# One matmul for two outputs of a spectral filter: 36 blocks in place of 48

## What is computed

```python
def _stu_conv(phi, u, n):
    sgn = jnp.where(jnp.arange(sl) % 2 == 0, 1.0, -1.0)
    ...
    U_plus = irfft(Vf[None, :, :, None] * Uf_p[:, :, None, :])[:, :sl]
    U_minus = irfft(Vf[None, :, :, None] * Uf_m[:, :, None, :])[:, :sl]
    U_minus = U_minus * sgn[None, :, None, None]

def _compute_spectral(u, sigma, phi, Mpp, Mpm):
    U_plus, U_minus = _stu_conv(phi, u, PADDED_SL)
    s = sigma ** SIGMA_POW
    out = jnp.einsum('btkd,k,kde->bte', U_plus, s, Mpp)
    return out + jnp.einsum('btkd,k,kde->bte', U_minus, s, Mpm)
```

## Time and profile before

| | us |
|---|---|
| median of three runs (3904.05 to 3920.32) | 3916.36 |
| the profiled execution, span from the first to the last instruction | 3932.8 |
| PE busy | 3385.7 |
| DVE busy | 2484.0 |
| POOL busy | 1702.7 |
| ACT busy | 1442.3 |
| matmuls of L1599, 3072 of them, busy | 507.5 |

### The profile page before, as it was taken

One profiled execution on the slowest core, in us unless ns is written; L12 is line 12 of the kernel. 1 busy time (PEld: TensorE's weight loads), 2 busy tenths in 40 slices (PEclk: granted clock), 3 DMA queues, 4 the chain that ended last, 5 costly groups with the idle time before them and its releaser, 6 DMA issues. The chain is left out here.

```text
span 3932.8 us, 69093 instructions
## 1 busy us (share of the span) xinstructions
PE 3385.7 (86%) x21387; PEld 2365.0 (60%) x21387; DVE 2484.0 (63%) x4247; ACT 1442.3 (37%) x2188; POOL 1702.7 (43%) x1424
## 2 busy tenths in 40 slices
PE   6336999999999999999999999999999569999998
PEld 1124555555555555555555555555555359898887
DVE  2346666676666767666766766667676556464646
ACT  0002333333333333333333333333333235454545
POOL 0464555555555555555555555555555320000000
PEclk8557999999999999999999999999999779999999
DMA  2524454445545544444554445455555624333333
GB/s 78 165 85 138 120 133 127 131 125 129 137 119 133 135 126 128 130 132 118 138 134 124 126 129 136 120 132 135 125 130 124 136 70 135 101 133 102 119 123 103
DMA packets 289629, 487.77 MB, mean 124 GB/s; under 512 B 95336, under 2 KB 113144, under 8 KB 289304
## 3 DMA queue, kind: packets, MB, share of 16 engines
q1 hardware_dynamic: 257160, 398.26, 36.8%
q0 software_dynamic: 32400, 88.52, 9.4%
HBM read 258.31 MB, written 23.27 MB: 72 GB/s over the span
## 5 line engine op out<-in xcount | busy, mean ns | idle before, releaser
L1108 ACT ACTIVATE attention_probs<-attention_pss 128x896 f32<-128x896 f32 (+4 forms) x768 | 623.0, 811 | 1320.9 <-PE attention_pss L957 1310.4
L1165 DVE TENSOR_REDUCE attention_mx<-attention_pss 128x2 f32<-128x1024 f32 (+3 forms) x520 | 525.5, 1022 | 377.8 <-PE attention_pss L970 208.1
L1041 PE MATMUL attention_psY<-attention_probs,attention_xt 128*64 128x128 f32 (+7 forms) x4386 | 733.5, 440 | 2.1 <-DMA attention_xt<-xt 1.8
L1283 POOL DMA_INDIRECT attention_gat<-table,attention_idx x585 | 559.8, 957 | 191.6 <-issue 118.8
L954 PE MATMUL attention_pss<-attention_QA,attention_KA 128*128 128x512 f32 (+4 forms) x1536 | 554.1, 416 | 49.5 <-ACT attention_probs L1108 43.7
L1696 DVE SCALAR_TENSOR_TENSOR spectral_eo<-spectral_psE,spectral_sig,spectral_eo 64x512 fp32r<-64x512 f32 x512 | 383.9, 750 | 263.8 <-ACT spectral_eo L1675 259.2
L1264 POOL TENSOR_TENSOR attention_nat_l<-attention_qk,attention_nat_h 128x512 fp32r<-128x512 f32 x260 | 425.3, 1636 | 259.3 <-ACT attention_nat_h L1127 259.3
L970 PE MATMUL attention_pss<-attention_nat_h 64*128 64x512 f32 (+2 forms) x1560 | 350.7, 451 | 201.7 <-DVE attention_mx L1165 198.2
L1599 PE MATMUL spectral_psE<-spectral_tz,spectral_up 128*128 128x256 f32 (+2 forms) x3072 | 507.5, 324 | 4.3 <-DVE spectral_eo L1696 4.3
L1256 POOL TENSOR_TENSOR attention_qk<-attention_tA,attention_tB 128x512 f32<-128x512 f32 x260 | 411.1, 1592 | 203.5 <-DVE attention_tB L1180 201.9
L1599 PEld LDWEIGHTS spectral_psE<-spectral_tz,spectral_up 128*128 128x128 f32 x3072 | 470.7, 188 | 44.9 <-DVE spectral_eo L1696 6.1
(11 more groups left out here) (194 smaller groups left out, 3862.4 us busy)
## 6 DMA issues: line engine op xcount, KB each, us to landing
attention_QA<-attention_nat_h SPq DMA_DIRECT2D x520, 128.0 KB
spectral_tz<-phis SPq DMA_DIRECT2D x128, 320.5 KB, 4.7
spectral_tz<-phis SPq DMA_DIRECT2D x128, 320.0 KB, 4.3
attention_xb<-xn SPq DMA_DIRECT2D x66, 512.0 KB, 4.0
attention_wt<-wsplit SPq DMA_DIRECT2D x66, 512.0 KB, 5.9
attention_KA<-attention_nat_h SPq DMA_DIRECT2D x260, 128.0 KB
attention_KB<-attention_nat_h SPq DMA_DIRECT2D x260, 128.0 KB
attention_KA<-attention_nat_l SPq DMA_DIRECT2D x260, 128.0 KB
```

The costliest lines, as they stand in the source:

```text
L1041: ins = pe.matmul(psY[C * half:C * half + C, c0:c1], xt[:, kt_, :], probs[:, q + c0:q + c1], start=first, stop=(j == NS - 1), skip_group_c ...
L1108: act.activation(probs[:, pstep[j]:pstep[j] + width], pss[:, slot, lead:lead + width], ACT.Exp, scale=float(E) ** -0.5).then_inc(s_act, 1)
L1165: ins = dve.tensor_reduce(mx_far[:, :, i - 4] if k0 else mx[:, :, i], scores, AX.X, ALU.max)
L1283: pool.indirect_dma_start(gat[:, n, :, :].rearrange("p q c -> p (q c)"), None, d.table.rearrange("r q c -> r (q c)"), bass.IndirectOffsetO ...
```

## The change

The two outputs that take their tokens from the same parity have the same stationary operand. One matmul now makes both of them: its moving operand is a stretch of the even taps' rows and one of the odd taps' rows, and its output is two runs in one PSUM bank. So that both fit a bank, it holds only half of the positions of each output. A unit `u = 2 * src + half` stands in the place of the output `e`: `half` 0 is positions 0 to 255, `half` 1 the rest. A unit of `half` 0 needs the token blocks 0 and 1, one of `half` 1 all four; the last block of each has 128 columns of each output, the others 256.

For this `tz` keeps the two tap parities in one row, `LAGS` apart, and the odd ones are read one element later where `src` is 0. `phases` gives the places in `eo` that the two halves of a bank belong to; `eo` itself and `mix_in` are as before. The number of instructions of ACT and DVE, their sizes, the loads and the semaphores with their counts are the same.

```diff
+LAGS = P + HB + 2
...
-        tz = sb("tz", [P, 2, 2, 2, P + HB + 1], F32R)
+        tz = sb("tz", [P, 2, 2, 2 * LAGS + 2], F32R)
...
+        def phases(k, u, rows, b):
+            src, half = u // 2, u % 2
+            flat = eo[rows, k % 2, :, :, b, 2 * P * half:2 * P * half + 2 * P].rearrange("q o p n -> q (o p) n")
+            return flat[:, 0:4:3, :] if src == 0 else flat[:, 1:3, :]
...
-                                sp.dma_start(tz[:, k % 2, part, odd, 0:n].bitcast(F32),
+                                sp.dma_start(tz[:, k % 2, part, odd * LAGS:odd * LAGS + n].bitcast(F32),
...
-                        for e in range(4):
-                            odd, p = e // 2, e % 2
-                            pe.wait_ge(s_lo, 64 * g + 4 * k + e + 1)
-                            src = p if not odd else 1 - p
-                            off = P + (1 if odd and p == 1 else 0)
+                        for u in range(4):
+                            src, half = u // 2, u % 2
+                            pe.wait_ge(s_lo, 64 * g + 4 * k + u + 1)
+                            wide = LAGS + 1 - src
                             for n, (x, y) in enumerate(((0, 0), (0, 1), (1, 0))):
-                                for a in range(4):
-                                    first = min(P * a, HB - 2 * P)
-                                    lag = off + first - P * a
-                                    ins = pe.matmul(psE[:, e, first:HB], up[:, x, src, a, :],
-                                                    tz[:, k % 2, y, odd, lag:lag + HB - first],
-                                                    start=(n == 0 and a == 0), stop=(n == 2 and a == 3))
+                                both = tz[:, k % 2, y, 0:2 * wide].rearrange("p (o n) -> p o n", o=2)
+                                for a in range(2 * half + 2):
+                                    first = max(P * a, 2 * P * half)
+                                    width = 2 * P * (half + 1) - first
+                                    lag = P + first - P * a
+                                    ins = pe.matmul(psE[:, u, :].rearrange("q (o n) -> q o n", o=2)[:, :, 2 * P - width:2 * P],
+                                                    up[:, x, src, a, :], both[:, :, lag:lag + width],
+                                                    start=(n == 0 and a == 0), stop=(n == 2 and a == 2 * half + 1))
                             ins.then_inc(s_full, 1)
...
-                                ins = act.activation(eo[rows, k % 2, e // 2, e % 2, b, :], psE[rows, e, :], ACT.Copy,
-                                                     scale=sig[rows, k:k + 1])
+                                ins = act.activation(phases(k, u, rows, b), psE[rows, u, :].rearrange("q (o n) -> q o n", o=2),
+                                                     ACT.Copy, scale=sig[rows, k:k + 1])
...
                                 ins = dve.scalar_tensor_tensor(
-                                    out=eo[other, k % 2, e // 2, e % 2, b, :], in0=psE[rows, e, :], scalar=sig[rows, k:k + 1],
-                                    in1=eo[rows, k % 2, e // 2, e % 2, b, :].bitcast(F32), op0=ALU.mult, op1=ALU.subtract)
+                                    out=phases(k, u, other, b), in0=psE[rows, u, :].rearrange("q (o n) -> q o n", o=2),
+                                    scalar=sig[rows, k:k + 1], in1=phases(k, u, rows, b).bitcast(F32),
+                                    op0=ALU.mult, op1=ALU.subtract)
```

More of the change, by code:

```diff
@@ L1670, in _ @@
                         act.wait_ge(s_mix, KF * g + k + 1)
-                        for e in range(4):
-                            act.wait_ge(s_full, 64 * g + 4 * k + e + 9)
+                        for u in range(4):
+                            act.wait_ge(s_full, 64 * g + 4 * k + u + 9)
                             for b in range(2):
                                 rows = slice(C * b, C * b + C)
-                                ins = act.activation(eo[rows, k % 2, e // 2, e % 2, b, :], psE[rows, e, :], ACT.Copy,
-                                                     scale=sig[rows, k:k + 1])
+                                ins = act.activation(phases(k, u, rows, b), psE[rows, u, :].rearrange("q (o n) -> q o n", o=2),
+                                                     ACT.Copy, scale=sig[rows, k:k + 1])
                             ins.then_inc(s_hi, 1)
@@ L1691, in _ @@
                     for k in range(KF):
-                        for e in range(4):
-                            dve.wait_ge(s_hi, 64 * g + 4 * k + e + 1)
+                        for u in range(4):
+                            dve.wait_ge(s_hi, 64 * g + 4 * k + u + 1)
                             for b in range(2):
```

## The result

| | before | after |
|---|---|---|
| median of the runs, us | 3917.97 (3904.05 to 3920.32, four) | 3885.34 (3872.60 to 3889.10, four) |
| span of the profiled execution, us | 3932.8 | 3881.3 |
| from the first `conv` matmul to the end, us | 722.8 | 684.9 |

The ratio is 0.9923, with a 95% interval of 0.9905 to 0.9941: 30 us faster, between 23 and 37. The forecast was 3874 with 42 us saved. So the time lies inside the stated range and the sign is right, but by these runs some 10 us of the saving are not there, more than this interval allows.

What follows compares the result with a forecast made beforehand. PE's matmul columns in `conv` were taken to bound the last stage: 46.7 us saved less 4.6 given back at the normalisation is 42.1, so 3916.4 becomes 3874 us. The range was 3860 to 3896 us.

Steps and rivals of the forecast that it cites:

- PE's columns bound the stage: In `conv`, 15,360 columns replace 16,896: 7.04 us against 7.77, a gain of 46.7 us over 64 filters.
- Two runs cost nothing: In `conv`, reading operands and writing narrow blocks' outputs as two runs priced at 0; range kept 107 ns per narrow block.
- The first and the second rival: Narrow two-run blocks pay 20 to 30 ns, 3890 to 3897 us (0.08); they fall to half rate, 3950 us (0.08).
- ACT, DVE and the loads: Writing two runs costs ACT and DVE 0 to 10 ns per instruction, hidden; loads keep 3 us of cover.
- The normalisation: Behind filter 9, PE's longer wait and a second gap give back 1.15 us per pass, 4.6 us in four.
- The sum: Last stage: 46.7 us from columns less 4.6 at the normalisation, 42.1 us saved, giving 3874 us.
- the clock would stay at 1.00 through the pass: Sign of a right forecast: TensorE's clock stays on its upper level of 2.4 GHz throughout each pass.
- The wait itself: PE's wait for DVE's normalisation before `conv` 10: some 1.25 us before the change, 1.95 us after it.

Runs made afterwards that it cites:

- split kernels: Normalisation split (statistics after filter 8, scaling after filter 10), in the changed kernel and the kernel before: 3866.58 and 3910.61 us, ratios 0.9872 and 0.9996.
- second trace of the changed kernel: The changed kernel run again with no edit, for more pairs of runs and another trace: 3879.62 us, ratio 0.9922 to the kernel before.
- the narrow last block: The kernel before with the last block of each output cut from 256 to 128 columns, without pairing: 3907.67 us, ratio 0.9979.
- the kernel before with the longer wait: The kernel before with six of sixteen statistics made twice, lengthening PE's wait behind filter 9: 3927.30 us, ratio 1.0012.
- the longer normalisation: The changed kernel with the first statistics made twice, so that DVE comes later: 3884.15 us, ratio 0.9934 to the kernel before.

## Why the prediction was right, and where it was not

- PE's columns bound the stage: right. The split kernels show 45.5 us for the columns; the sum had 46.7. Between them lie 0.3 us per pass. They may be `mix_in`'s: its matmuls take 2 and 3 ns more than before (395 and 285 ns in the changed kernel, 393 and 282 in the earlier trace rows), 24 ns for its ten, 16 times; this was not tested by itself.
- Two runs cost nothing: right, on the read and on the output. A narrow block takes 282 ns. The Trainium skill, Advanced Engine Details and Errata, section PSUM Cachelines, would have any non-contiguous access slow matmuls down; the trace doesn't agree with that sentence for runs of 128 float32 values, and is in line with the one behind it on pairs. The first and the second rival, 16% together, fall by this row.
- ACT, DVE and the loads: right. Their durations are the same, and PE never waited for a load.
- The normalisation: the mechanism was right, the size was not. Forecast: 0.70 + 0.45 = 1.15 us given back per pass. Against the split kernels, the wait cost 1.4 us per pass before; after, it cost 2.5 where the clock stayed, 1.1 more and as forecast, with 0.67 in the first wait (1.76 against 1.09) and 0.48 in the second, and 3.8 where it fell, 2.4 more. The step that failed is the one that priced a longer wait at its own length: the fall of the clock behind it costs another 1.3 us. With the clock lost in two passes this is 7 us in all, in four 9.7; forecast were 4.6.
- The sum: 45.5 - 9.7 = 35.8 us over the four passes when the clock falls in each, as in the second trace of the changed kernel; 33.5 were measured in that trace's stage. What remains, 2.3 us, lies between the passes, where each new pass starts with a stretch at the lower clock that varies from trace to trace: the granted clock between two passes is 0.94, 0.89 and 0.94 in the trace of before, with 86.4 us in all, and 0.88 three times in the second trace, with 88.6. So the stage falls short of the forecast 42.1 us by 4.2 us in the first trace (37.9 saved: 1.2 by the columns, 2.4 by the clock, the rest between the passes) and by 8.6 in the second (1.2, 5.1 and 2.3). The runs give 30 us by the ratio, between 23 and 37, and 31, between 19 and 42.

The prediction had said that the clock would stay at 1.00 through the pass, and no rival had it fall. The wait itself was worked out as 1.95 us; what was not asked is what a wait of that length does to the engine that waits. The trace of before had rows on both sides of it. Its waits of 1.09 us in the middle of a pass leave the clock at 1.00. Between the first pass and the second, PE waits 2.04 us, works for half a microsecond, waits 2.25 us more, and its clock falls (a line of the timeline, then windows as above):

```profile
3371.88 1.23 PE L1620 MATMUL spectral_psE<-kept_ident,spectral_un 128*128 128x128 f32 x5 [2.25 <-issue]
```

```profile
3371.00:3373.00 2.00, 1.12 (x6) 1.12 (x6) 0.56 (x1) 0.00 (x0) 0.00 (x0) 0.64 0.00 0
3373.00:3375.00 2.00, 2.00 (x11) 2.00 (x11) 0.00 (x0) 1.02 (x1) 0.00 (x0) 0.50 0.96 203
```

These two waits stand close together, so they don't tell what a single one of 1.95 us would do, but they were reason to give the fall a rival of its own. That the time still lies in the range is in part luck: the range reached that far up for noise and for a price of the two runs, and what used it was the clock.

## What to carry to other kernels

When an engine is made faster, the waits that stay fixed in time grow by what it gains; ask of each what a longer wait brings with it, and not only how long it is. Moving part of another engine's work away from such a wait (here DVE's reciprocal and sixteen scalings, 3.9 us, two filters later) took another 10 to 15 us off the stage. Idle columns are worth cutting only down to the size that still covers a weight load; below that, pair blocks that share their stationary operand.

## What the runs showed of the hardware

The clock of TensorE fell behind a single wait in the midst of full work, and how often goes with the wait's length. It fell behind a wait of 0.4 us in none of four passes, 0.8 us none of four, 1.1 us none of eight (the kernel before, and with the narrow last block), 1.76 to 1.78 us six of eight, 1.85 us four of four, 2.3 us four of four, 3.8 us four of four. I had not expected it behind waits this short, nor that it could come late: in the second pass of the changed kernel's trace (columns as above) PE waits, works on for a microsecond at the upper level, has 1.9 us and more at the lower one, and is back at 1.00 within 2 us more.

```profile
3459.80:3461.60 1.80, 0.04 (x1) 0.00 (x0) 1.72 (x4) 1.76 (x3) 0.00 (x0) 1.00 0.99 299
3461.60:3463.10 1.50, 1.49 (x6) 0.92 (x6) 1.48 (x2) 0.03 (x1) 0.00 (x0) 0.84 0.98 383
3463.10:3465.00 1.90, 1.85 (x5) 1.57 (x6) 1.83 (x3) 1.36 (x2) 0.00 (x0) 0.50 0.08 32
3465.00:3467.00 2.00, 2.00 (x10) 1.61 (x8) 1.94 (x4) 0.00 (x0) 0.00 (x0) 0.74 0.00 0
3467.00:3470.70 3.70, 3.70 (x22) 3.18 (x21) 2.77 (x4) 2.73 (x4) 0.00 (x0) 1.00 0.00 0
```

Elsewhere it came sooner: within a quarter of a microsecond of PE's return in the first pass of the kernel before with the longer wait, and in the longer normalisation's first pass while PE still waited (clock 0.50 from 3267.20 to 3268.70, where PE returns). So the row of the wait alone does not show its cost; the clock column of the stretch behind it does.
